# Attention tails: half of the weighted values ahead of the third exponential, half behind the next unit's scores

## The reference

```python
q = jnp.einsum('bsd,hdk->bhsk', queries, Wq) + bq[None, :, None, :]
k = jnp.einsum('bsd,hdk->bhsk', keys, Wk) + bk[None, :, None, :]
v = jnp.einsum('bsd,hdk->bhsk', values, Wv) + bv[None, :, None, :]
scores = jnp.einsum('bhsk,bhtk->bhst', q, k) / jnp.sqrt(jnp.float32(HEAD_DIM))
probs = jax.nn.softmax(scores, axis=-1)
attended = jnp.einsum('bhst,bhtk->bhsk', probs, v)
...
normed = (attended - mean) * jax.lax.rsqrt(var + LN_EPS)
return normed * gamma + beta
```

## Time and profile before

| what | us |
|---|---|
| runs | 871.19, 861.65, 864.48 |
| median | 864.48 |
| profiled execution, span from first to last instruction | 882.9 |
| profiled execution, time besides its span | none recorded |
| attention stretch, first scores of heads 0, 1 to the last output turn | 480.31 to 644.68 |

### The profile page before, as it was taken

One profiled execution on the slowest core, in us unless ns is written; L12 is line 12 of the kernel. 1 busy time (PEld: TensorE's weight loads), 2 busy tenths in 40 slices (PEclk: granted clock), 3 DMA queues, 4 the chain that ended last, 5 costly groups with the idle time before them and its releaser, 6 DMA issues.

```text
span 882.9 us, 14436 instructions
## 1 busy us (share of the span) xinstructions
PE 648.7 (73%) x4155; PEld 413.5 (47%) x4155; DVE 588.8 (67%) x1604; ACT 426.3 (48%) x906; POOL 410.5 (46%) x436
## 2 busy tenths in 40 slices
PE   4498788888788678899977777777632216999991
PEld 2143344344334357679963343434321114878881
DVE  2767888879897957886856595947556675443343
ACT  2295876786789443554433453524321012444442
POOL 3316436478677354513544666772200003656641
PEclk9598998989989859999998997959865556999996
DMA  6587997656767226536762101000030001111115
GB/s 168 181 270 261 331 306 246 208 204 199 227 228 228 80 61 190 170 114 171 197 199 111 39 19 30 22 1 12 1 119 1 0 0 27 40 43 43 43 34 152
DMA packets 97477, 109.79 MB, mean 124 GB/s; under 512 B 12597, under 2 KB 80889, under 8 KB 97018
## 3 DMA queue, kind: packets, MB, share of 16 engines
q1 hardware_dynamic: 68986, 84.87, 29.8%
q0 software_dynamic: 6592, 13.51, 5.4%
q10 hardware_dynamic: 21824, 10.49, 4.1%
HBM read 84.38 MB, written 24.44 MB: 123 GB/s over the span
## 4 chain that ended last, share of the span: by engine, by line
PE 37%; DVE 28%; ACT 10%; issue 7%; DMA 6%; another core or an unknown queue 4%; POOL 3%; SPq 2%; DVEq 1%; ACTq 1%; POOLq 0%
PE PS L2065 6%; DMA oh<-index 4%; PE PS L2076 3%; DVE nmx L1570 3%; PE PS L2276 3%; DVE oh L1424 2%; PE PS L2181 2%; PE PS L1995 2%; PE PS L2153 2%; PE PS L2155 2%; PE PS L2030 2%; PE PS L1990 1%; PE PS L2204 1%; PE PS L2252 1%
## 5 line engine op out<-in xcount | busy, mean ns | idle before, releaser
L644 POOL DMA_INDIRECT xs<-xn,row x64 | 70.7, 1104 | 54.1 <-PE PS L2065 35.2
L693 POOL DMA_INDIRECT yb<-ys,yrow x64 | 60.9, 952 | 73.3 <-PE PS L2065 37.1
L780 POOL DMA_INDIRECT xg<-xrows,tok x39 | 37.5, 961 | 103.2 <-DVE tok L1771 91.6
L1990 PE MATMUL PS<-oh,T 128*128 128x512 bf16 x240 | 71.3, 409 | 16.9 <-ACT oh L910 15.9
L1424 DVE TENSOR_SCALAR oh<-oh,pcol 128x2048 bf16<-128x2048 bf16 x80 | 66.0, 825 | 18.6 <-DMA oh<-index 17.3
L1995 PE MATMUL PS<-oh,T 128*32 128x512 bf16 x960 | 72.5, 411 | 0.0
L2065 PE MATMUL PS<-xT,wgu 128*96 128x128 f32 x512 | 68.8, 278 | 4.9 <-ACT xT L954 2.5
L909 ACT ACTIVATE oh<-oh,pcol 128x512 bf16<-128x512 bf16 x80 | 57.8, 722 | 15.6 <-DMA oh<-index 15.6
L2065 PEld LDWEIGHTS PS<-xT,wgu 128*96 128x96 f32 x512 | 60.5, 166 | 7.4 <-issue 3.8
L2004 PE MATMUL PS<-ident,gs 128*128 128x128 f32 x320 | 55.2, 298 | 9.7 <-ACT vv L931 9.1
L910 ACT ACTIVATE oh<-oh,pcol 128x512 bf16<-128x512 bf16 x80 | 57.8, 722 | 2.6
(11 more groups left out here) (406 smaller groups left out, 1642.9 us busy)
## 6 DMA issues: line engine op xcount, KB each, us to landing
oh<-index SPq DMA_DIRECT2D x80, 512.0 KB
oh<-index SPq DMA_DIRECT2D x80, 128.0 KB
x<-xs SPq DMA_DIRECT2D x128, 64.0 KB
ys<-y ACTq DMA_DIRECT2D x64, 128.0 KB
w<-in_w SPq DMA_DIRECT2D x8, 384.0 KB, 5.7
xs<-nil SPq DMA_DIRECT2D x48, 64.0 KB
xs<-nil SPq DMA_DIRECT2D x7, 320.0 KB
wg1r<-in_wg SPq DMA_DIRECT2D x1, 2048.0 KB, 8.7
```

What stands on the lines that cost most here:

```text
L644: pool.indirect_dma_start(xs[:], bass.IndirectOffsetOnAxis(ap=row0[:, QT * b + t, k:k + 1], axis=0), xn1[:, b % 2, t, :], None).then_inc(s ...
L693: pool.indirect_dma_start(yb[:, b % 2, t, k, :], None, ys[b // 2][:], bass.IndirectOffsetOnAxis(ap=yrow0[:, QT * b + t, k:k + 1], axis=0))\
L1990: pe.matmul(o, T2[:, b % 2, p, n // NK, :], oh[:, slot, GH, :], start=(p == 0), stop=False, skip_group_check=True)
```

## The change

The output accumulation is split. In slot 1, TensorE goes on from the scores of heads 0, 1 to V2d and the values of heads 2, 3 (new semaphore ot_part). In slot 2, behind the third exponential, it first issues the next unit's scores of heads 2, 3 (`first_scores`), then the values of heads 0, 1. The Kb2 score stays in slot 0 and waits for the copy of the unit before. ScalarE copies the output after the next unit's exponential of heads 2, 3 (`read_output`), which itself waits for ot_part. The output turn follows the scores of slot 0. The maxima start one slot earlier.

```diff
-MAX_FIRST = -4
+MAX_FIRST = -5
...
+            def read_output(u):
+                act.wait_ge(s["ot_ps"], u + 1)
+                if u >= 1:
+                    act.wait_ge(s["side_ps"], SIDE["ott", (u - 1) // NG, (u - 1) % NG] + 1)
+                act.copy(ots[:], PS[:, 5, :]).then_inc(s["ot_ev"], 1)
+
             def exponentials(b, g, part):
                 u = NG * b + g
                 if part == 0:
                     if u >= 1:
-                        act.wait_ge(s["ot_ps"], u)
+                        act.wait_ge(s["ot_part"], u)
                     act.wait_ge(s["s_b"], u + 1)
                     act.activation(Ex[:, 2:4, :], PS[:, 0:2, :], ACT.Exp, scale=INV_SQRT).then_inc(s["e_b"], 1)
+                    if u >= 1:
+                        read_output(u - 1)
                     act.wait_ge(s["s_c"], u + 1)
...
-                if part == 2:
-                    act.wait_ge(s["ot_ps"], u + 1)
-                    if u >= 1:
-                        act.wait_ge(s["side_ps"], SIDE["ott", (u - 1) // NG, (u - 1) % NG] + 1)
-                    act.copy(ots[:], PS[:, 5, :]).then_inc(s["ot_ev"], 1)
...
+                    if b == B - 1 and q == PERIOD:
+                        read_output(B * NG - 1)
...
+            def first_scores(b, g):
+                pe.wait_ge(s["mx_used"], N_MAX * b + MAX_UNITS.index(("turn", g, 0)) + 1)
+                for h in range(2, 4):
+                    last = pe.matmul(PS[:, h - 2, :], Kbd[:, b, g, h, 0:P], qf[:, b % 2, g, :], start=True, stop=True)
+                last.then_inc(s["s_b"], 1)
+
+            def weighed(b, g, heads):
+                for h in heads:
+                    last = pe.matmul(PS[32 * h:32 * h + 32, 5, :], V1[:, b, g * P + 32 * h:g * P + 32 * h + 32],
+                                     Ex[:, h, :], start=False, stop=True, skip_group_check=True)
+                return last
+
             def scores(b, g, part):
...
                 if part == 0:
-                    pe.wait_ge(s["mx_used"], N_MAX * b + MAX_UNITS.index(("turn", g, 0)) + 1)
                     if u == 0:
+                        first_scores(0, 0)
                         pe.wait_ge(s["zeros_made"], 4)
-                    if u:
+                    else:
                         pe.wait_ge(s["ot_ev"], u)
-                    for h in range(2, 4):
-                        last = pe.matmul(PS[:, h - 2, :], Kbd[:, b, g, h, 0:P], q, start=True, stop=True)
-                    last.then_inc(s["s_b"], 1)
                     pe.matmul(PS[:, 5, :], Kb2[:, b, g, :], q, start=True, stop=True).then_inc(s["s_c"], 1)
                 if part == 1:
...
                     last.then_inc(s["s_a"], 1)
+                    pe.wait_ge(s["e_c"], u + 1)
+                    pe.matmul(PS[:, 5, :], V2d[:, b, g, :], Ex2[:], start=True, stop=False, skip_group_check=True)
+                    weighed(b, g, range(2, 4)).then_inc(s["ot_part"], 1)
                 if part == 2:
                     pe.wait_ge(s["e_a"], u + 1)
-                    pe.wait_ge(s["e_c"], u + 1)
-                    pe.matmul(PS[:, 5, :], V2d[:, b, g, :], Ex2[:], start=True, stop=False, skip_group_check=True)
-                    for h in range(GH):
...
-                    last.then_inc(s["ot_ps"], 1)
+                    if u + 1 < B * NG:
+                        first_scores(*divmod(u + 1, NG))
+                    weighed(b, g, range(2)).then_inc(s["ot_ps"], 1)
 
             for r in range(FRONT_FIRST, PERIOD * (B - 1) + BACK_LAST + 1):
+                for b in range(B):
+                    q = r - PERIOD * b
+                    if 0 <= q < PERIOD:
+                        scores(b, q // 3, q % 3)
                 for b in range(B):
                     q = r - PERIOD * b
                     if q in (3, 6, 9, 12):
                         turn_output(b, q // 3 - 1)
                 for b in range(B):
-                    q = r - PERIOD * b
-                    if 0 <= q < PERIOD:
-                        scores(b, q // 3, q % 3)
-                    maxima(b, q - MAX_FIRST - 1)
+                    maxima(b, r - PERIOD * b - MAX_FIRST - 1)
```

More of the change, by code:

```diff
@@ L400, in seq_kernel @@
             zeros_made k_ps k_ev v_ps v_ev key_sums kbd_ready gathered0 gathered1 gathered2 gathered3 gathered4 gathered5 scattered0 scattered1 scattered2 x2_ready xn2_ready side_ps side_read
-            q_made mx_ps mx_used nm_ready s_a s_b s_c e_a e_b e_c ot_ps ot_ev
+            q_made mx_ps mx_used nm_ready s_a s_b s_c e_a e_b e_c ot_part ot_ps ot_ev
             att_normed att_scaled beta_added x3_ready var3 rs3 xn3_ready xrows_out
@@ L2149, in scores @@
                     last.then_inc(s["s_a"], 1)
+                    pe.wait_ge(s["e_c"], u + 1)
+                    pe.matmul(PS[:, 5, :], V2d[:, b, g, :], Ex2[:], start=True, stop=False, skip_group_check=True)
+                    weighed(b, g, range(2, 4)).then_inc(s["ot_part"], 1)
                 if part == 2:
                     pe.wait_ge(s["e_a"], u + 1)
-                    pe.wait_ge(s["e_c"], u + 1)
-                    pe.matmul(PS[:, 5, :], V2d[:, b, g, :], Ex2[:], start=True, stop=False, skip_group_check=True)
-                    for h in range(GH):
-                        last = pe.matmul(PS[32 * h:32 * h + 32, 5, :], V1[:, b, g * P + 32 * h:g * P + 32 * h + 32],
-                                         Ex[:, h, :], start=False, stop=True, skip_group_check=True)
-                    last.then_inc(s["ot_ps"], 1)
+                    if u + 1 < B * NG:
+                        first_scores(*divmod(u + 1, NG))
+                    weighed(b, g, range(2)).then_inc(s["ot_ps"], 1)
             for r in range(FRONT_FIRST, PERIOD * (B - 1) + BACK_LAST + 1):
+                for b in range(B):
+                    q = r - PERIOD * b
+                    if 0 <= q < PERIOD:
+                        scores(b, q // 3, q % 3)
                 for b in range(B):
```

## The result

The changed kernel takes 876.64 us (median of 4) against 867.84 for the kernel before (median of 4): a ratio of 1.0131, interval 1.0086 to 1.0176. The ratio is of the fast runs alone; one of the four runs before, 878.48, lies 2.0% above the fastest and counts as slow, so the medians are 8.8 us apart and the ratio says 11.4. The two profiled executions differ outside the attention phase too, so their spans (875.2 after, 882.9 before) can't be set against each other; the phase can.

What follows compares the result with a forecast made beforehand. No engine is full; units wait on a ring of hand-overs. Phase 130.45 + 27.0 + 0.4 = 157.9, plus 2.5 and 10 gives 170.4 against 164.4, so 864.5 + 6 = 870.5, given as 870; range 852 to 886.

Steps and rivals of the forecast that it cites:

- the forecast's own case: Whole kernel: between 8 us faster and 8 us slower, likeliest 6 us slower; chance 0.45.
- the bare unit: Last batch, a unit without side work: 5.7 us against 8.45 before, 2.75 less; sign: a unit near 6 us.
- the held exponentials: ScalarE: sign that exponentials of line 1019 are released not by scores but by ScalarE itself behind a query.
- The catch of ScalarE's order: ScalarE's queue: next exponential stands behind side work, copy and Kb2 behind it; front batches 130.45 us against 130.7.
- The price of a half: TensorE, value passes of two heads: 1.00 us each, so the split adds 1.0 us to each of 16 units.
- the walk: Attention phase followed unit by unit without disturbances: front batches 130.45 us, last batch 27.0, phase 157.9 with 0.4 added.
- theory 1 of e2: Queue order: without the split only third and fourth units gain, 1 to 6 us less than the changed kernel, 870 to 876.
- The rest of the edits: Maxima one slot earlier add no work; at the start query 1 comes behind two maxima, taken as 0.4 us.
- The disturbances: Attention phase, added to the walk: 2.5 us for NMp waits and 10 us for time at the low clock.
- The faster rival: Held exponentials in front batches cost half as much, other work going on meanwhile: 18 us less, 852.5; chance 0.20.
- The slower rival: Clock: dense TensorE runs after long gaps at 1.2 GHz cost 27 us, not 10: 887.5; chance 0.35 with the third rival.
- The third rival: Values of heads 2, 3 come behind the third exponential anyway: 4 us, 874; within the slower rival's 0.35.

Runs made afterwards that it cites:

- e1: Changed kernel with the next unit's exponential and the output copy in slot 2 ahead of its side work: 849.17 us, ratio 0.9799 to the kernel before.
- e3: Changed kernel with only the output copy back in slot 2 ahead of its side work, exponential left in slot 0: 851.82 us, ratio 0.9825.
- e7: Kernel of e1 with only the next exponential in slot 2, the output copy staying in slot 0 behind the side work: 866.17 us, ratio 1.0017.
- e2: Changed kernel with the value passes of all four heads together in slot 2, V2d staying in slot 1: 867.63 us, ratio 1.0002.
- e10: Kernel of e4 with V2d alone moved ahead of the third exponential, all four heads' values together in slot 2: 847.31 us, ratio 0.9808.
- e6: Kernel of e4 with V2d and the values of heads 2, 3 moved into slot 1 ahead of the third exponential: 866.16 us, ratio 0.9997.
- e4: Kernel before with one edit alone, the maxima starting one slot earlier (MAX_FIRST = -5): 856.22 us, ratio 0.9899.
- e9: Changed kernel with eight unused matmuls before TensorE's wait for the copy, at borders into third and fourth units of batches 0 to 2: 872.19 us, ratio 1.0103.
- e5: Kernel of e1 without the split, all four heads' values together in slot 2 behind the next scores: 845.75 us, ratio 0.9772.

## Why the prediction was right, and where its size was off

The direction and the range held: 6 us slower was forecast, 8.8 by the medians and 11.4 by the ratio were measured (7.5 to 15.3 by its interval). With 1.3% the outcome lies past the edge of the forecast's own case, which had 0.45, and in the class given 0.35. Of the signs that the prediction named, the halves, the bare unit, the held exponentials and the waits came; the stretches ahead of and behind the phase did move, most likely by the one execution of the kernel before, as said above.

- **The catch of ScalarE's order** was right, and the runs show it to be the main cause. The third unit was walked as 12.35 us and took 12.5 in batch 1, the last batch as 27.0 and took 26.4, the bare unit as 5.7 and took 5.6. e1, e3 and e7 tell the links apart: it is the copy behind the side work, with Kb2 and all of TensorE's queue behind it, that decides. The exponential ahead alone takes 10 us off by the medians, the copy alone 25, both 27. The clock rose with it, so these gains hold a share of the clock.
- **The price of a half**, 1.00, measured 0.99, and not 0.86. That term stood in the walk with its full size. What theory 1 of e2 had too small is how much of it lies on the path: the changed kernel without the split has a ratio 1.3% lower, and between e10 and e6 the split costs 1.9%, its full price. The 0.43 between the passes of V2d is not half of its row, which is 0.95 / 2 = 0.475; it follows from the row's 1.02 less 0.59 for one pass in the trace. No term of the sum uses it.
- **The step that was mis-sized** is "The rest of the edits. Maxima one slot earlier: no work added", taken as 0.4 us lost. Alone it gains 1.0% (e4). No run has the changed kernel with the maxima in their old place, so it is not shown that the gain is whole there. If it is, the rest of the change costs 20 us, where the sum has 5.6, and the forecast came as near to the 11 as it did because two misses of opposite sign met, which is luck.
- **The disturbances** were put at 12.5 us (2.5 and 10). The three front batches took 148.9 where the walk says 130.45: 18.5. The third units, where the catch stands by itself, hold 0.6 of that, the second 2.9, the first 5.5 and the fourth 9.4. Of the first units the one of batch 1 took 9.9 us at a clock of 1.00, for 9.75 in the walk; those of batches 0 and 2 took 12.4 and 12.5 at 0.79 and 0.77, so there the excess goes with the low clock. Of the fourth, a part that the walk left out is plain in VectorE's and ScalarE's timeline at the end of batch 1:

```profile
560.16 5.25 DVE L1132 TENSOR_SCALAR xn<-XR,mvc,rstdc 128x128 f32<-128x128 f32 x4
```
```profile
566.68 0.58 ACT L1056 COPY xn3T<-PS 128x512 f32<-128x512 f32 x1 [5.33 <-PE PS L2201]
567.16 1.03 ACT L1025 ACTIVATE Ex<-PS 128x1024 f32<-128x1024 f32 x1
```

  VectorE took 5.25 us to write xn3 while POOL was adding gathered rows; the transpose and the copy of xn3T waited for it, and the attention exponential behind that copy. This unit took 17.0 us for the 10.65 of the walk.
- **The faster rival** (holds half hidden) fell: TensorE's 30 us of waits for the copy are there. **The slower rival**, the clock, does not explain the difference between the two kernels: its mean is 0.88 as before. But the gaps of the new order have a price through it: e1 and e3 have the same TensorE work at 0.98 and 0.99, and e9 shows about 5 us of it.
- **The third rival** fell by its mechanism: the values of heads 2, 3 start right behind V2d in every unit. By its outcome it is half true: in nine of the 16 units they start 0.04 to 0.58 us behind the end of the third exponential, all of them units where V2d took 1.37 to 1.91 us for its 1.02 at full clock, so there no value pass ran beside the exponential.
- Where the maxima's gain (e4) comes from, VectorE's lead or another source, was not tried.

## What to carry to other kernels

When a step is pulled ahead on one engine, pull its partners on the other engines ahead too: here the next unit's scores went a slot earlier on TensorE, while their exponential and the copy that frees the bank stayed behind side work on ScalarE, and two moved steps in that queue (e1) turned 1.3% slower into 2.0% faster. Do not split matmuls that run side by side in column strips without timing a half: here two strips took 0.99 us and four 1.00. And try the small edit of a bundle alone, since the best single part of this one (maxima a slot earlier, 1.0%) was hidden by the rest; the version without the split and with ScalarE's order mended (e5) beats the kernel before by 2.3%.

## What the runs showed of the hardware that was not expected

Unused matmuls of 102 columns in a wait of TensorE, 1.9 us of them at a border, went with a mean granted clock of the phase of 0.93 for 0.88 and shortened the six periods by 4.7 us; a wait of 2.84 us without them was followed by a stretch at 0.50. And one VectorE step of four scalings, 1.11 us in the kernel before with POOL idle (first row), took 5.25 us in the changed kernel, shown above, while POOL made additions back to back; one of them is the second row.

```profile
605.30 1.11 DVE L1127 TENSOR_SCALAR xn<-XR,mvc,rstdc 128x128 f32<-128x128 f32 x4
```
```profile
561.37 1.27 POOL L715 TENSOR_TENSOR yb<-yb 128x512 f32<-128x512 f32 x1
```

That POOL is the cause is argued from the two timelines; no run tried it.
